# Second attention stage: a new table of steps for two heads on every engine, and a table of places for the neighbouring norms

## The chip, the cores and the metric

The kernel runs on one core of a Trainium2 chip. The metric is the device time of one execution in microseconds (us). A core has TensorE (PE, with its weight loads as PEld), VectorE (DVE), ScalarE (ACT), GpSimd (POOL) and SyncE (SP), each with an instruction stream of its own that it works off in order. A step that depends on another engine waits for a semaphore, and everything behind it in its stream waits with it.

## The reference

Six sublayers work on x of 2048 tokens by 256: a routed feed-forward, an attention, the same feed-forward again, a gated feed-forward, a second attention, the gated feed-forward again. Each reads a layer norm of x and adds its result to x. The change concerns the second attention:

```python
q = (x @ Wq.T).reshape(B, T, H, Dh)      # T 2048, H 16 heads, Dh 128
k = (x @ Wk.T).reshape(B, T, H, Dh)
v = (x @ Wv.T).reshape(B, T, H, Dh)
q = _apply_rope(q, cos, sin)
k = _apply_rope(k, cos, sin)
scores = jnp.einsum('bthd,bshd->bhts', q, k) * scale
scores = jnp.where(causal[None, None], scores, -jnp.inf)
attn = jax.nn.softmax(scores, axis=-1)
y = jnp.einsum('bhts,bshd->bthd', attn, v).reshape(B, T, H * Dh)
return y / 3.0 @ Wo.T
```

## The kernel before

The program runs six stages one behind the other; the fifth is `Attention1`, between two stages of the gated feed-forward. Every matrix product is made of three matmuls of two halves, a high one rounded and a low one that holds the rest (`products`, lines 166 to 168; the scores, line 1277).

The work of a head is cut into steps. The queries come in 16 tiles t of 128 rows, in 8 pairs g; the keys of tile t come in t // 4 + 1 chunks c of up to 512 columns. In the letters of the tables:

- p, `project`: q and k of a pair (12 matmuls of 256 columns into one of two ring banks), then four VectorE operations for the rotation (from line 2625);
- f, `finish`: ScalarE copies out the high halves (lines 2530, 2531), VectorE the low halves (2635, 2636);
- S, `score`: on TensorE three matmuls (1277) into one of four banks; on VectorE the chunk's peak (1290; 2323 for the last chunk of a tile, which is masked too), and then the tile's bias (2331);
- x, `exp`: ScalarE's exponential of a chunk (1311), which needs the bias of the whole tile and frees the bank. A chunk's scores wait for the exponential of four chunks earlier;
- T, `turn`: ScalarE rounds a chunk of probabilities (2305), GpSimd takes the rest (2336), SyncE transposes both by DMA (2346). There are eight rooms for this, and three rooms for the turned probabilities of a pair;
- s, `pv`: products (g, j) of a pair's probabilities with block j of the values, into one of two y banks;
- y, `round`: ScalarE's high half of y (2553) and VectorE's low half (2666);
- o, `out`: TensorE's product with Wo (6 matmuls), ScalarE's scaling by the softmax sums (2562), GpSimd's addition to x (2705);
- v, `values`, once for two heads (12 matmuls into the ring; 2538, 2655); i, `invert`, the reciprocals of the sums; b and u, `bound` and `share`, scales for values and Wo (2642; 2646, 2650), which pass through GpSimd (2682); q, w, l the splitting of weights, and Q, W, L on SyncE their loads.

A head has 40 score chunks, 25 of 512 columns, 7 of 384, 7 of 256 and one of 128, with three matmuls each, and 72 products of three matmuls, 64 over 256 columns and 8 over 128.

The order is written out by hand. `TABLE` (line 2079) holds for each engine a string of letters that stands for two heads; `plan_order` reads it ten times over, and each letter takes the next step of its kind. `LEAD` says with which step each letter begins in the first reading, so it shifts a kind of work against the others: `"s": -21` on `pe` lets the products trail the scores. The waits come from the data and the rooms and are placed with each step, whatever the order. `with_norms` then puts in the steps of two neighbouring norms: `stats`, `scale` and `flip` of the last chunk of this stage's own norm, which fall into head 0, `next_stats`, `next_scale` and `next_flip` of the first two chunks of the following stage's norm, and `ahead`, two pieces of its weights, which fall into head 15. It finds their places by rules. `pe_score` is called for each `score`:

```python
if old := self.old_chunk[key]:
    pe.wait_ge(*self.p_done[old])
```

## Time and profile before

| | us |
|---|---|
| median of three runs (1786.37 to 1788.04) | 1787.68 |
| the profiled execution | 1790.02 |
| its span, first to last instruction | 1788.2 |
| TensorE busy in the span | 1673.8 |
| VectorE busy | 1380.6 |
| ScalarE busy | 1246.9 |
| GpSimd busy | 1081.2 |
| mean granted TensorE clock | 0.989 |

The second attention takes two thirds of the span: its first matmul starts at 476.53 us, the next stage's first at 1687.63. Busy times of TensorE have modelled ends, and a matmul's window overlaps the next one's, so its starts say more than its durations.

### The profile page before, as it was taken

What the parts mean: (1) busy time and instruction counts of PE and PEld (TensorE: products, weight loads), DVE (VectorE), ACT (ScalarE), POOL (GpSimd) and SP (SyncE); (2) the same over time, 40 slices, a digit from 0 to 9 for tenths busy, and PEclk for the clock granted to TensorE, in tenths of its full rate; (3) what the DMA queues carried; (4) which work ended last, traced back from release to release, by engine and by line L of the source; (5) the groups of instructions that cost most, each with busy time, mean ns of one, the idle gap of its engine ahead of it and who ended that gap; (6) DMA issues with size and microseconds to landing.
All of it is one profiled execution on the core that took longest, in us unless ns stands there. A gap on an engine that the chain in (4) does not pass through costs nothing.

```text
span 1788.2 us, 37269 instructions
## 1 busy us (share of the span) xinstructions
PE 1673.8 (94%) x11566; PEld 1440.7 (81%) x11566; DVE 1380.6 (77%) x3611; ACT 1246.9 (70%) x3255; POOL 1081.2 (60%) x1098
## 2 busy tenths in 40 slices
PE   6998988999789999999999999999999999999899
PEld 4777876778778788888888878878888887887788
DVE  7358865475698898988989889898888988989453
ACT  4335642345378879779788897887978888788742
POOL 2633114553247767767685786776778678677732
PEclk9999999999999999999999999999999999999999
DMA  8843047640048867786696876868779587786700
GB/s 294 242 79 48 13 163 230 150 100 1 15 79 149 127 119 136 119 145 122 117 157 97 153 124 121 138 118 136 131 120 152 100 145 125 119 142 121 134 21 28
DMA packets 636133, 215.96 MB, mean 121 GB/s; under 512 B 587296, under 2 KB 622752, under 8 KB 635808
## 3 DMA queue, kind: packets, MB, share of 16 engines
q1 hardware_dynamic: 625568, 200.71, 58.3%
q0 software_dynamic: 10368, 12.85, 4.4%
q8 instruction: 95, 1.56, 0.4%
q14 instruction: 102, 0.84, 0.2%
HBM read 51.06 MB, written 19.80 MB: 40 GB/s over the span
## 4 chain that ended last, share of the span: by engine, by line
PE 60%; DVE 17%; ACT 8%; issue 7%; DMA 4%; POOL 3%; SPq 0%; ACTq 0%; POOLq 0%; DVEq 0%
PE phase_scores L1277 16%; PE phase_y L166 6%; PE phase_y L168 6%; PE phase_y L167 6%; ACT phase_p L1311 4%; PE phase_ring L166 4%; PE phase_ring L168 4%; PE phase_ring L167 4%; DVE phase_peaks L1290 2%; DVE phase_ring L2628 2%; PE phase_up_ps L166 2%; DMA y_rows<-phase_out,phase_rows 2%; DVE phase_crossed L2626 2%; DVE phase_crossed L2625 2%; PE phase_up_ps L168 2%
## 5 line engine op out<-in xcount | busy, mean ns | idle before, releaser
L2336 POOL TENSOR_TENSOR phase_split<-phase_p,phase_split 128x512 f16<-128x512 f32 (+3 forms) x640 | 650.4, 1016 | 183.1 <-ACT phase_split L2305 139.3
L1311 ACT ACTIVATE phase_p<-phase_scores,phase_bias 128x512 f32<-128x512 f32 (+3 forms) x680 | 417.7, 627 | 75.8 <-DVE phase_bias L2331 52.9
L2305 ACT ACTIVATE phase_split<-phase_p 128x512 f16<-128x512 f32 (+3 forms) x640 | 338.7, 578 | 4.8 <-DMA phase_pt<-phase_split 3.3
L1290 DVE TENSOR_REDUCE phase_peaks<-phase_scores 128x1 f32<-128x512 f32 (+1 forms) x408 | 267.1, 668 | 69.1 <-PE phase_scores L1277 66.3
L166 PE MATMUL phase_y<-phase_pt,phase_v_hi 128*128 128x256 f16 (+1 forms) x1152 | 308.0, 269 | 2.7 <-DMA phase_pt<-phase_split 2.0
L167 PE MATMUL phase_y<-phase_pt,phase_v_hi 128*128 128x256 f16 (+1 forms) x1152 | 307.6, 267 | 0.0
L168 PE MATMUL phase_y<-phase_pt,phase_v_lo 128*128 128x256 f16 (+1 forms) x1152 | 304.2, 267 | 0.0
L1277 PE MATMUL phase_scores<-phase_k_hi,phase_q_hi 128*128 128x512 f32 (+3 forms) x640 | 255.4, 399 | 38.4 <-ACT phase_p L1311 25.7
L2705 POOL TENSOR_TENSOR sb_x<-sb_x,phase_part 128x512 f32<-128x512 f32 x128 | 164.0, 1282 | 127.4 <-ACT phase_part L2562 121.7
L1277 PE MATMUL phase_scores<-phase_k_hi,phase_q_lo 128*128 128x512 f32 (+3 forms) x640 | 233.1, 364 | 0.0
L1277 PE MATMUL phase_scores<-phase_k_lo,phase_q_hi 128*128 128x512 f32 (+3 forms) x640 | 233.0, 364 | 0.0
L1277 PEld LDWEIGHTS phase_scores<-phase_k_hi,phase_q_hi 128*128 128x128 f32 x640 | 121.5, 190 | 75.5 <-ACT phase_p L1311 31.7
L166 PEld LDWEIGHTS phase_y<-phase_pt,phase_v_hi 128*128 128x128 f16 x1152 | 112.2, 97 | 53.0 <-issue 35.7
L166 PE MATMUL phase_ring<-sb_xt_hi,late_qk_hi 128*128 128x256 f32 x512 | 146.2, 286 | 0.0
L167 PE MATMUL phase_ring<-sb_xt_lo,late_qk_hi 128*128 128x256 f32 x512 | 142.8, 279 | 0.0
L168 PE MATMUL phase_ring<-sb_xt_hi,late_qk_lo 128*128 128x256 f32 x512 | 142.7, 279 | 0.0
L1311 ACT ACTIVATION_READ_ACCUMULATOR phase_p<-phase_scores,phase_bias 128x1 f32 x680 | 141.2, 208 | 0.0
L1277 PEld LDWEIGHTS phase_scores<-phase_k_hi,phase_q_lo 128*128 128x128 f32 x640 | 121.6, 190 | 17.4
L1277 PEld LDWEIGHTS phase_scores<-phase_k_lo,phase_q_hi 128*128 128x128 f32 x640 | 122.4, 191 | 7.9
L168 PEld LDWEIGHTS phase_y<-phase_pt,phase_v_lo 128*128 128x128 f16 x1152 | 112.8, 98 | 11.6
L167 PEld LDWEIGHTS phase_y<-phase_pt,phase_v_hi 128*128 128x128 f16 x1152 | 113.4, 98 | 9.3
L2323 DVE CUSTOM_DVE_ANT_0 phase_scores<-phase_scores,sb_hide,phase_peaks 128x256 f32<-128x256 f32 x192 | 113.4, 591 | 5.9 <-DVE phase_peaks L2320 0.3
(313 smaller groups left out, 4485.8 us busy)
## 6 DMA issues: line engine op xcount, KB each, us to landing
phase_pt<-phase_split SPq DMA_TRANSPOSE x640, 3.3
y_rows<-phase_zero SPq DMA_DIRECT2D x16, 512.0 KB, 7.6
phase_e_up<-expert_up SPq DMA_DIRECT2D x16, 352.0 KB, 4.2
phase_e_dn<-expert_down SPq DMA_DIRECT2D x16, 256.0 KB, 5.4
xn_rows<-phase_ln_xn SPq DMA_DIRECT2D x8, 512.0 KB, 2.9
sb_x<-y_rows POOLq DMA_DIRECT2D x8, 512.0 KB, 6.2
late_raw_qk<-qk SPq DMA_DIRECT2D x16, 256.0 KB, 3.2
phase_logits_t<-expert_up SPq DMA_DIRECT2D x8, 352.0 KB, 4.2
```

Source lines behind the costliest of these rows:

```text
L166: pe.matmul(out, left_hi[c], r_hi, start=first and c == 0, stop=False)
L167: pe.matmul(out, left_hi[c], r_lo, start=False, stop=False)
L168: done = pe.matmul(out, left_lo[c], r_hi, start=False, stop=last and c == n - 1)
L1277: done = pe.matmul(self.scores[:, at:at + n], a, b, start=k == 0, stop=k == len(pairs(n)) - 1)
L1290: dve.tensor_reduce(peak, scores, AX.X, ALU.max).then_inc(*self.peaked.one)
L1311: act.activation(self.p_room(act, key)[:, 0:width], self.scores[:, at:at + width], ACT.Exp, bias=self.bias[:, t % 2:t % 2 + 1], accum_out= ...
L2305: act.activation(hi, value, ACT.Copy).then_inc(*self.t_hi.one)
L2323: dve.tensor_tensor_reduce(scores, scores, self.core.hide[:, CH - w:], 1.0, before, ALU.add, ALU.max, top).then_inc(*self.peaked.one)
L2336: pool.tensor_tensor(lo, value, hi, ALU.subtract).then_inc(*self.t_lo.one)
L2625: dve.tensor_tensor(self.crossed[0:32], both[32:64], self.wide(slice(96, 128), g), ALU.mult)
L2626: dve.tensor_tensor(self.crossed[32:64], both[0:32], self.wide(slice(64, 96), g), ALU.mult).then_inc(*self.crossing.one)
L2705: pool.tensor_tensor(rows, rows, self.part[:, g % 2], ALU.add).then_inc(*self.added.one)
```

## The change

It replaces the five strings of `TABLE` and the numbers of `LEAD`, and puts a table `PLACES` in place of the rules of `with_norms`. Each string holds the same letters, as often as before, in another order; what each engine executes stays the same. A row of `PLACES` names a step and the norm steps that follow it directly (-1 is the last head). The strings are cut here to the first row of `pe`:

```diff
 TABLE = {
-    "pe": ("SSpSsssSpssssssssssssSSSSpsssssSSSsvSooSpSSsSsvssoSSSpssssSsSSsvvoSsSSpssSSsssSssssvvoSSSSsssssssssSSSSsvvoSSSSp"
...
+    "pe": ("sSpssSSsssSssoSspsssSSsssSvosSsSsSsssSsssssspSosSsvSSSssvSSposSSvsSSsssssoSSvsSpSsvSssssSovsSSSssSsspSSSSosvsSsSS"
...
 LEAD = {
-    "pe": {"S": 0, "s": -21, "p": 2, "v": 0, "o": -2, "b": 1},
-    "act": {"x": 0, "T": -1, "f": 1, "y": -2, "v": 0, "o": -2, "l": 0, "q": 1, "w": 1},
-    "dve": {"f": 1, "S": 0, "i": 0, "p": 2, "y": -2, "v": 0, "b": 1, "u": 1},
-    "pool": {"T": -2, "o": -2, "l": 0, "q": 1, "w": 1, "b": 1},
-    "sp": {"T": -5, "L": 1, "Q": 2, "W": 2},
+    "pe": {"S": 0, "s": -27, "p": 3, "v": 0, "o": -3, "b": 1},
+    "act": {"x": -10, "T": -12, "f": 0, "v": 0, "y": -4, "o": -5, "q": 1, "w": 1, "l": 0},
+    "dve": {"S": -2, "p": 2, "f": 0, "v": 0, "y": -3, "i": -2, "b": 1, "u": 0},
+    "pool": {"T": 4, "o": -1, "q": 1, "w": 1, "l": 0, "b": 1},
+    "sp": {"T": 26, "Q": 2, "W": 2, "L": 2},
+}
+PLACES = {
+    "pe": ((("project", 0, 1), ("flip", 3, 0), ("flip", 3, 1)),
+           (("pv", -1, 6, 1), ("next_flip", 0, 0)),
+           (("pv", -1, 7, 7), ("next_flip", 0, 1)),
+           (("out", -1, 7), ("next_flip", 1, 0), ("next_flip", 1, 1)),),
...
+    "dve": (((), ("stats", 3)),
+           (("project", 0, 0), ("scale", 3)),
+           (("finish", 0, 0), ("flip", 3, 0), ("flip", 3, 1)),
...
+    "sp": (),
 }
@@ with_norms @@
+        for after, *steps in PLACES[engine]:
+            at = order.index((after[0], after[1] % NH, *after[2:])) + 1 if after else 0
+            order[at:at] = steps
         return order
```

VectorE in the middle of the stage, head 7 (odd), from the first peak of tile 8 on. L2625 to L2630 are the rotation of a projection, L2666 is the low half of y, L2323 and L2331 end the tile. Before:

```order
L1290 TENSOR_REDUCE phase_peaks<-phase_scores 128x1
L2642 TENSOR_SCALAR phase_bound<-phase_ring 128x1
L2625 TENSOR_TENSOR phase_crossed<-phase_ring,late_rope 32x512
L2626 TENSOR_TENSOR phase_crossed<-phase_ring,late_rope 32x512
L2628 TENSOR_TENSOR phase_ring<-phase_ring,late_rope 64x512
L2630 TENSOR_TENSOR phase_ring<-phase_ring,phase_crossed 64x512
L1290 TENSOR_REDUCE phase_peaks<-phase_scores 128x1
L2666 TENSOR_TENSOR phase_y_lo<-phase_y,phase_y_hi 128x256
L2320 TENSOR_REDUCE phase_peaks<-phase_peaks 128x1
L2323 ISA phase_scores,phase_top<-phase_scores,sb_hide,phase_peaks 128x256
L2323 ISA phase_top 128x1
L2331 TENSOR_SCALAR phase_bias<-phase_top 128x1
```

With the change (lines behind `with_norms` lie six lower, so L2619 is L2625):

```order
L1290 TENSOR_REDUCE phase_peaks<-phase_scores 128x1 x2
L2660 TENSOR_TENSOR phase_y_lo<-phase_y,phase_y_hi 128x256
L2314 TENSOR_REDUCE phase_peaks<-phase_peaks 128x1
L2317 ISA phase_scores,phase_top<-phase_scores,sb_hide,phase_peaks 128x256
L2317 ISA phase_top 128x1
L2325 TENSOR_SCALAR phase_bias<-phase_top 128x1
L1327 TENSOR_REDUCE phase_inv<-phase_sums 128x1
L1329 RECIPROCAL phase_inv<-phase_inv 128x1
L2660 TENSOR_TENSOR phase_y_lo<-phase_y,phase_y_hi 128x256
L2619 TENSOR_TENSOR phase_crossed<-phase_ring,late_rope 32x512
L2620 TENSOR_TENSOR phase_crossed<-phase_ring,late_rope 32x512
```

The projection, which stood between the first and the second chunk of tile 8, follows the tile and two low halves of y.

TensorE in head 7, from product (3, 7), the last of pair 3, on: `phase_pt` with `phase_v` are products, `phase_wo` with `phase_y` an output, `phase_ring` a projection. Before:

```order
L166 MATMUL phase_y<-phase_pt,phase_v_hi 128x128
L167 MATMUL phase_y<-phase_pt,phase_v_hi 128x128
L168 MATMUL phase_y<-phase_pt,phase_v_lo 128x128
L166 MATMUL phase_y<-phase_wo_hi,phase_y_hi 128x256
L167 MATMUL phase_y<-phase_wo_lo,phase_y_hi 128x256
L168 MATMUL phase_y<-phase_wo_hi,phase_y_lo 128x256
L166 MATMUL phase_y<-phase_wo_hi,phase_y_hi 128x256
L167 MATMUL phase_y<-phase_wo_lo,phase_y_hi 128x256
L168 MATMUL phase_y<-phase_wo_hi,phase_y_lo 128x256
L166 MATMUL phase_y<-phase_wo_hi,phase_y_hi 128x256
L167 MATMUL phase_y<-phase_wo_lo,phase_y_hi 128x256
L168 MATMUL phase_y<-phase_wo_hi,phase_y_lo 128x256
```

With the change:

```order
L166 MATMUL phase_y<-phase_pt,phase_v_hi 128x128
L167 MATMUL phase_y<-phase_pt,phase_v_hi 128x128
L168 MATMUL phase_y<-phase_pt,phase_v_lo 128x128
L166 MATMUL phase_ring<-sb_xt_hi,late_qk_hi 128x256
L167 MATMUL phase_ring<-sb_xt_lo,late_qk_hi 128x256
L168 MATMUL phase_ring<-sb_xt_hi,late_qk_lo 128x256
L166 MATMUL phase_ring<-sb_xt_hi,late_qk_hi 128x256
L167 MATMUL phase_ring<-sb_xt_lo,late_qk_hi 128x256
L168 MATMUL phase_ring<-sb_xt_hi,late_qk_lo 128x256
```

Before, the output of pair 2 and then that of pair 3 follow the last product of pair 3, and tile 13's scores come behind them. Now a projection of head 8 follows, three products of pair 4 come behind it, then tile 13; pair 3's output stands behind product (4, 9).

VectorE at the start of the stage: L241 and L245 are the statistics of the last norm chunk, L2642 the bound, L2646 and L2650 the share, L2625 the first projection. Before:

```order
L241 BN_STATS phase_ln_stats<-sb_x 128x6 x4
L245 BN_AGGR phase_ln_mv<-phase_ln_stats 128x2 x4
L2642 TENSOR_SCALAR phase_bound<-phase_ring 128x1
L2646 TENSOR_SCALAR phase_spread<-phase_v_scale 128x1
L2650 RECIPROCAL phase_wo_scale<-phase_spread 128x1
L2625 TENSOR_TENSOR phase_crossed<-phase_ring,late_rope 32x512
L2626 TENSOR_TENSOR phase_crossed<-phase_ring,late_rope 32x512
```

With the change:

```order
L241 BN_STATS phase_ln_stats<-sb_x 128x6 x4
L245 BN_AGGR phase_ln_mv<-phase_ln_stats 128x2 x4
L2636 TENSOR_SCALAR phase_bound<-phase_ring 128x1
L2619 TENSOR_TENSOR phase_crossed<-phase_ring,late_rope 32x512
L2620 TENSOR_TENSOR phase_crossed<-phase_ring,late_rope 32x512
L2622 TENSOR_TENSOR phase_ring<-phase_ring,late_rope 64x512
L2624 TENSOR_TENSOR phase_ring<-phase_ring,phase_crossed 64x512
L281 TENSOR_TENSOR phase_ln_tmp<-phase_ln_rstd 128x4
```

The share step has gone behind later work, and the norm's scale follows the first projection.

## Rows read from the trace of the kernel before

**Rows 1.** The page, busy us, share of the span and instructions of each engine.
```profile
PE 1673.8 (94%) x11566; PEld 1440.7 (81%) x11566; DVE 1380.6 (77%) x3611; ACT 1246.9 (70%) x3255; POOL 1081.2 (60%) x1098
```

**Rows 2.** Windows: busy us (instructions) by engine, granted clock, DMA share, GB/s.
```profile
524.00:1664.00 1140.00, 1096.85 (x8128) 956.56 (x8127) 986.49 (x2610) 953.12 (x2611) 831.22 (x793) 1.00 0.76 129
```

**Rows 3.** The chain that ended last: start us, us, what.
```profile
652.08 1.92 PE phase_scores L1277 x9
...
1540.97 1.92 PE phase_scores L1277 x9
```

**Rows 4.** Timeline of TensorE: start us, us, engine, line, operation, count [idle before].
```profile
1089.74 0.27 PE L166 MATMUL phase_y<-phase_pt,phase_v_hi 128*128 128x256 f16 x1
...
1090.61 0.27 PE L168 MATMUL phase_y<-phase_pt,phase_v_lo 128*128 128x256 f16 x1
...
1091.25 0.28 PE L1277 MATMUL phase_scores<-phase_k_hi,phase_q_hi 128*128 128x256 f32 x1
...
1091.60 0.40 PE L1277 MATMUL phase_scores<-phase_k_hi,phase_q_hi 128*128 128x512 f32 x1
...
1092.29 0.28 PE L1277 MATMUL phase_scores<-phase_k_hi,phase_q_hi 128*128 128x256 f32 x1
```

**Rows 5.** Waits of TensorE, 524 to 1664: us in total, times, longest.
```profile
PE phase_scores L1277 <- ACT phase_p L1311: 25.1, 54, 1.0
...
PE phase_y L166 <- DVE phase_y_lo L2666: 17.3, 25, 1.0
```

**Rows 6.** Timeline of TensorE, waits in one pair of heads.
```profile
1035.88 0.38 PE L166 MATMUL phase_y<-phase_wo_hi,phase_y_hi 128*128 128x256 f32 x1 [1.03 <-DVE phase_y_lo L2666]
...
1037.53 0.50 PE L1277 MATMUL phase_scores<-phase_k_hi,phase_q_hi 128*128 128x512 f32 x1 [0.70 <-ACT phase_p L1311]
...
1057.59 0.38 PE L166 MATMUL phase_y<-phase_wo_hi,phase_y_hi 128*128 128x256 f32 x1 [0.58 <-DVE phase_y_lo L2666]
...
1102.48 0.47 PE L1277 MATMUL phase_scores<-phase_k_hi,phase_q_hi 128*128 128x512 f32 x1 [0.98 <-ACT phase_p L1311]
```

**Rows 7.** Timeline of VectorE and ScalarE around those waits.
```profile
1032.08 0.68 DVE L2625 TENSOR_TENSOR phase_crossed<-phase_ring,late_rope 32x512 f32<-32x512 f32 x1
...
1034.94 0.56 DVE L1290 TENSOR_REDUCE phase_peaks<-phase_scores 128x1 f32<-128x384 f32 x1
...
1036.51 0.15 DVE L2331 TENSOR_SCALAR phase_bias<-phase_top 128x1 f32<-128x1 f32 x1
...
1056.30 0.38 ACT L2553 ACTIVATE phase_y_hi<-phase_y 128x256 fp32r<-128x256 f32 x1
...
1057.12 0.41 DVE L2666 TENSOR_TENSOR phase_y_lo<-phase_y,phase_y_hi 128x256 fp32r<-128x256 f32 x1
```

**Rows 8.** Timeline: tile 13 of head 7, last score, reduction, first exponential.
```profile
1061.13 0.28 PE L1277 MATMUL phase_scores<-phase_k_hi,phase_q_lo 128*128 128x256 f32 x1
...
1062.18 0.49 DVE L2323 CUSTOM_DVE_ANT_0 phase_scores<-phase_scores,sb_hide,phase_peaks 128x256 f32<-128x256 f32 x1
...
1062.95 0.69 ACT L1311 ACTIVATE phase_p<-phase_scores,phase_bias 128x512 f32<-128x512 f32 x1 [0.18 <-DVE phase_bias L2331]
```

**Rows 9.** Timeline of TensorE and VectorE, start of the stage.
```profile
487.19 0.47 PE L1277 MATMUL phase_scores<-phase_k_hi,phase_q_hi 128*128 128x128 f32 x1 [7.31 <-DVE phase_k_lo L2636]
...
480.21 0.15 DVE L2646 TENSOR_SCALAR phase_spread<-phase_v_scale 128x1 f32<-128x1 f32 x1 [2.12 <-POOL phase_v_scale L2682]
...
480.59 0.68 DVE L2625 TENSOR_TENSOR phase_crossed<-phase_ring,late_rope 32x512 f32<-32x512 f32 x1
```

**Rows 10.** Timeline and waits of TensorE, end of the stage.
```profile
1670.86 0.56 PE L166 MATMUL phase_y<-phase_wo_hi,phase_y_hi 128*128 128x256 f32 x1 [1.96 <-DVE phase_y_lo L2666]
...
PE phase_y L166 <- DMA phase_pt<-phase_split: 2.0, 1, 2.0
```

**Rows 11.** Line 2346, the transposes: ns min/median/max, and who waited for them.
```profile
L2346 SPq DMA_TRANSPOSE phase_pt<-phase_split x640: 1171/1259/2544, 492.1 to 1680.5; - x160
...
  ACT phase_split L2305: 3.3, 7
```

More of the change, by code:

```diff
@@ new lines @@
+    "act": ("xTxoyTTTxxTxxTfToTfxxTyTxxxfxToTTTxfxyTxxxxTfvTTxxTToyxxTlyfovTxxvTTxTxTxxoyfvxxTTxTovTyxTxqTxfTTTvxxxxToyvTxxxT"
+           "xTTTTTxxxTTxvfToyTxxxxTfTxToyfTTwxxTfTTxoTxxTfxxTTxxTTTxyTxyTxoTxlfoyxTxxTTxoqyfTxxyTTTxoxTxTxTofTyxxxTxTTTxx"),
+    "dve": ("SfSifpSyiSSiifpSSifSSiuySpSiSifSviSypSSfSSivySvSpSiSySfSvSiSiSyvpSSfSviSSSSivySSSiSpSSiSfvSypiSfpSySfipSiSfiSiSp"
+           "SSiSbfSiSiSSySiypSSfSypSSiSfySiSySpSSSiSfiySSSiSpSSiSySpSS"),
+    "pool": "TTTloTTTTToTTTTTTTqTTTTToToTTTTTTTTToTTTTwTTToTTToTTTTTTTTToloTTTqToTTTTTooTTTTTTTTTTTTTTTTboTTTToToTo",
@@ L2089 @@
+    "sp": "TTTTTTTTTTTTTTTTTQTTTTTTTTTTTTTTTTTTTTTTTTTTLTTTTTQTTTTWTTTTTTTTTTTTTTTTTTTTTTTTTTTLT",
 }
 LEAD = {
[5 rows of a table removed]
[5 rows of a table added]
+}
[4 more added lines that the diff above has]
+           (("out", -1, 7), ("next_flip", 1, 0), ("next_flip", 1, 1)),),
+    "act": ((("finish", 0, 0), ("scale", 3), ("flip", 3, 0), ("flip", 3, 1)),
+           (("exp", -1, 13, 0), ("next_scale", 0)),
+           (("round", -1, 6), ("next_flip", 0, 0), ("ahead", 0), ("ahead", 1)),
+           (("out", -1, 6), ("next_flip", 0, 1)),
+           (("round", -1, 7), ("next_scale", 1), ("next_flip", 1, 0)),
+           (("out", -1, 7), ("next_flip", 1, 1)),),
+    "dve": (((), ("stats", 3)),
+           (("project", 0, 0), ("scale", 3)),
+           (("finish", 0, 0), ("flip", 3, 0), ("flip", 3, 1)),
+           (("score", -1, 12, 1), ("next_stats", 0)),
+           (("round", -1, 4), ("next_scale", 0)),
+           (("invert", -1, 15), ("next_stats", 1), ("next_flip", 0, 0)),
+           (("round", -1, 6), ("next_flip", 0, 1), ("next_scale", 1)),
+           (("round", -1, 7), ("ahead", 0), ("ahead", 1), ("next_flip", 1, 0), ("next_flip", 1, 1)),),
+    "pool": ((("bound", 0), ("stats", 3)),
+           (("turn", -1, 11, 2), ("next_stats", 0)),
+           (("out", -1, 4), ("next_stats", 1)),),
+    "sp": (),
@@ L2238, in with_norms @@
     def with_norms(self, engine, order):
-        def after(anchor, *steps):
-            if anchor in order:
-                order[order.index(anchor) + 1:order.index(anchor) + 1] = steps
-        late, h = NCH - 1, NH - 1
-        score = {"pe": "score", "act": "exp", "dve": "score"}.get(engine)
-        if engine in ("dve", "pool"):
-            order.insert(0, ("stats", late))
-        if engine in ("act", "dve"):
-            after((score, 0, 1, 0), ("scale", late))
-            at = order.index(("round", h, G - 1))
-            order[at:at] = [("ahead", m) for m in range(2)]
-        if engine in ("pe", "act", "dve"):
-            flips = [("flip", late, 0), ("flip", late, 1)]
-            if engine == "act" and order.index(("finish", 0, 2)) < order.index(("exp", 0, 2, 0)):
-                at = order.index(("finish", 0, 2))
-                order[at:at] = flips
-            else:
-                after((score, 0, 2, 0), *flips)
-        for c in AHEAD:
-            flips = [("next_flip", c, k) for k in range(HK)]
-            if engine == "dve":
-                later = [(score, h, NT - 1, NCH - 1)] * c
-                after(max([("round", h, 2 * c + 5), *later], key=order.index), *flips)
-                after(max([("round", h, 2 * c + 4), *later], key=order.index), ("next_scale", c))
-                after(("round", h, 2 * c + 3), ("next_stats", c))
-            elif engine == "act":
-                later = [(score, h, NT - 1, NCH - 1)] * c
-                after(max([("round", h, 2 * c + 5), *later], key=order.index), *flips)
-                after(max([("round", h, 2 * c + 4), *later], key=order.index), ("next_scale", c))
-            elif engine == "pool":
-                after(max([("out", h, 2 * c + 2)] + [("turn", h, NT - 1, NCH - 1)] * c, key=order.index), ("next_stats", c))
-            elif engine == "pe":
-                after(("out", h, 2 * c + 4), *flips)
+        for after, *steps in PLACES[engine]:
+            at = order.index((after[0], after[1] % NH, *after[2:])) + 1 if after else 0
+            order[at:at] = steps
         return order
```

11 lines of the change are left out of this document (3 added, 8 removed).

## The prediction

> **What bounds the kernel now.** I began with the busy shares: TensorE is busy 94% of the span, VectorE 77%, ScalarE 70% [rows 1]. They are averages over six stages, so I cut the span: in the second attention stage, from 524 to 1664 us, TensorE is busy 1096.85 of 1140 us, VectorE 986, ScalarE 953, GpSimd 831, at a granted clock of 1.00 [rows 2]. The stage repeats itself every two heads. In the chain of waits the same piece of scores comes at 652.08 and, six pairs of heads later, at 1540.97 [rows 3]: 148.15 us a pair.
>
> Is that TensorE's limit? By busy time almost. But the ends of matmuls are modelled and overlap their successors, so I counted from start to start in a stretch without waits. A product of probabilities and values takes 0.109 us (eight of them between 1089.74 and 1090.61); a score matmul of 256 columns takes 0.117 (three from 1091.25), one of 512 columns 0.23 (three from 1091.60) [rows 4]. I give 0.175 to 384 columns, 0.055 to half a product, and 0.117 to the projections, values and outputs, which have 256 columns of the same type too. A pair of heads has 384 whole and 48 half products, 150, 42, 42 and 6 scores of 512, 384, 256 and 128 columns, 288 matmuls of projections and values and 96 of outputs, all counted in the code. That is 41.9 + 2.6 + 34.5 + 7.4 + 4.9 + 0.6 + 33.7 + 11.2, about **137 us of streaming**. So TensorE loses about **11 us in each pair of heads**, 85 us over the 7.7 pairs from 524 to 1664.
>
> Where? The waits view of that stretch charges TensorE's idle time to ScalarE's exponentials (25.1 us, 54 times) and to VectorE's low half of y (17.3 us, 25 times) [rows 5]; idle time between modelled ends is less than what the starts lose. One pair shows the pattern [rows 6]: at 1035.88 an output step waits 1.03 us for the low half of y, at 1037.53 a score 0.70 for the bank that an exponential must free, at 1057.59 an output again, at 1102.48 a score.
>
> A rule of the Trainium skill bears on this. First the rows: TensorE's idle time by its busy row is 43 us in the stretch [rows 2], by starts it is 85. The Trainium skill, Perfetto Trace Analysis, section Identifying the Most-Contended Engine, says that matmul busy time is no good measure of how near the limit TensorE is, because pipelined matmuls look smaller in the trace. By the busy row the steady part could give back at most 43 us, half of what I look for below. The count of starts sides with the page.
>
> **The change, part by part.** Every engine executes the same instructions; only their order moves. So each term is a wait.
>
> *Steady part.* (a) VectorE had head 7's sixth projection inside tile 8, before its second chunk: four operations from 1032.08 on, so that chunk's peak starts at 1034.94 and the tile's bias at 1036.51 [rows 7]. The waits at 1035.88 and 1037.53 hang on it. In the new order the projection stands behind the tile and behind pair 7's low half. (b) Pair 3's output stood right behind pair 2's, 0.7 us of TensorE work behind its own pair's last product, while the round trip over ScalarE's copy (0.38 us) and VectorE's subtraction (0.41) [rows 7] costs about 1.2 us even with both free (my estimate: the two, and three crossings between engines like the 0.18 ahead of the exponential [rows 8], partly overlapped). Over the 16 outputs of a pair of heads, the work between last product and output is 0.7, 0.7, 1.4, 1.6, 1.8, 1.8 and 2.1 us for the seven shortest in the old order; in the new one 2.1, 2.1, 2.5, 2.9, then 4 and more. (c) The work between a tile's last score and the score that needs its first exponential was 1.9 us at its shortest (tile 8 to 9 of odd heads, the place of (a)); that place has 4.0 now. Tile 13 to 14 goes the other way, from 2.9 to 2.0 (even heads) and 2.2 (odd). That chain costs 2.4: the last score starts at 1061.13 and lasts 0.12, the exponential ends at 1063.64 [rows 8]. This leaves 0.4 and 0.2 us to wait.
>
> I also laid ScalarE's and VectorE's own work, in order, against TensorE's work between each event and the step that needs its outcome. The old order overruns by up to 1.6 us on ScalarE and 2.1 on VectorE, at the places of the waits; in the new one I find none above 0.1 beside tile 13's. Fetches of weights are moved past transposes in SyncE's queue, but each is still issued several tiles before its use; I cost them at nothing, and without that cover each would cost its landing once a head.
>
> What is left: 0.6 us for tile 13 and about 2 us a pair of slips that no distance explains, 2.7 in all. The bounds are 0.5 (no slips) and half of today's 11. Gain 8.4 x 7.7 = **64.7 us**.
>
> *Start.* TensorE waits 7.31 us before the first score at 487.19; VectorE stood 2.12 us of that at the share step, for GpSimd, and began the first projection at 480.59 [rows 9]. Now only the bound step stands before it, so it can begin at about 478.1. In return the last norm chunk's scale and flips come before the second projection's low halves, on ScalarE and VectorE too, and the scores behind them. I take **2.4** gained, nearly the whole of those 2.5 us, since the flips are only moved; bounds -4 and +6.
>
> *End.* Output 5 of the last head stood directly behind its last product and waited 1.96 us [rows 10]; it has 4.0 us of work ahead of it now. The last output, which had output 6 and two flips ahead of it, now stands directly behind the last product and pays the round trip of 1.2. The wait of 2.0 us for the last transposes [rows 10] stays, since the same 12.1 us of TensorE work lie between the last score and the product that needs them. **0.8** gained; bounds -3 and +4.
>
> Sum: 64.7 + 2.4 + 0.8 = 67.9. The profiled execution took 1790.0 us, so 1722.1; the median of the runs is 2.3 lower, so **1720 us**.
>
> On the floor of 137 us the rows say 0.23 us for 512 columns. The Trainium skill, TensorE: Matmul & The Clock Gate, section Back-to-back issue gap, gives 131 ns sustained. By it the 150 wide scores of a pair would cost 15 us less, so TensorE would not be at its limit even after the change. The rows decide; nothing of the sum rests on this.
>
> **The rivals.** *Half comes back (0.19).* The distances use durations of undisturbed rows, and a wait that goes makes the next engine late: VectorE would be busy 92% of a 140 us period. If half of the loss stays, the gain is 5.5 x 7.7 = 42, so 1746. For it: several places of the new order have under 0.4 us to spare. Against: all of today's large waits sit at places that are covered now.
>
> *Nothing comes back (0.04).* The 11 us could be TensorE's own, from switching between kinds of work; the new order switches 150 times a pair, the old 111. Then 1788. Against: the score of 256 columns behind another kind at 1091.25 pays nothing [rows 4].
>
> *Slower (0.05).* The products trail the scores by six steps more. There are three rooms for turned probabilities, so SyncE's transpose of tile 8 waits for product (1, 3) of the same head, with all later transposes behind it. TensorE's work from tile 8's last score to that product grows from 8.8 to 10.4 us in odd heads and from 7.6 to 9.2 in even ones. The way to the transpose is about 4.5: 2.4 to the exponential's end, then ScalarE's split and GpSimd's. SyncE's wait so grows to 5.9 and 4.7 us. ScalarE may be eight splits ahead, at 1.26 us a transpose [rows 11] a cover of 10 us; but it has already been caught seven times, for 3.3 us in all [rows 11]. If the waits reached TensorE in full, 10.6 + 2.7 would replace 11: 2.3 x 7.7 = 18 us slower, 1806. It decides once such a wait and the backlog behind it pass those 10 us.
>
> **How the numbers follow.** The forecast's case gets 0.72 and reaches from 1703 (0.5 left a pair) to 1740 (5 left). With most of the half case the range is 1703 to 1752; outside lie the cases nothing and slower, 0.09, a third of the half case and a little below, under 0.2 together. Faster by over 0.2% (about what a measurement of this kernel can tell from no change) 0.91; within it 0.04; slower 0.05.
>
> **What would show it.** Right: the scores' piece returns every 140 us instead of 148; TensorE's waits for exponentials and y are under 12 us in the steady part instead of 42; its DMA share goes from 0.76 to about 0.80, VectorE to 92%; at the start VectorE's first projection begins near 478. Wrong: a period above 144, ScalarE's splits waiting for transposes by tens of us, or TensorE waiting for transposes in every head.

## The result: 1722.0 us, and the profile after

The changed kernel takes 1721.99 us (median of 4 runs, 1718.1 to 1724.86), the kernel before 1787.12 (4 runs, 1786.37 to 1788.04). The ratio is 0.9635, with a 95% interval of 0.9617 to 0.9652. The forecast was 1720.0 in a range of 1703 to 1752. The profiled execution took 1724.86 us, and its rows are these.

The page of the changed kernel: busy us, share of the span and instructions of each engine; the chain that ended last, by engine.

```profile
PE 1648.0 (96%) x11566; PEld 1418.2 (82%) x11566; DVE 1373.5 (80%) x3611; ACT 1238.2 (72%) x3255; POOL 1081.6 (63%) x1098
...
PE 83%; DVE 8%; ACT 3%; issue 3%; DMA 2%; POOL 1%; SPq 0%; ACTq 0%; POOLq 0%; DVEq 0%
```

The busy times of VectorE, ScalarE and GpSimd are those of before within 1% [rows 1], as only the order moves. The steady part of the second attention, as windows and as TensorE's and SyncE's waits:

```profile
524.00:1600.00 1076.00, 1070.96 (x8128) 934.54 (x8127) 978.59 (x2611) 945.46 (x2613) 834.60 (x795) 1.00 0.79 137
```

```profile
PE phase_scores L1277 <- ACT phase_p L1311: 5.0, 3, 3.8
```

```profile
SPq L2340 <- POOL phase_split L2330: 501.4, 451, 6.7
SPq L2338 <- PE phase_y L168: 43.8, 22, 4.8
```

The waits for the low half of y are gone from this stretch, and of those for exponentials 5.0 us are left where 25.1 were [rows 5]. All three of these stand at 1584.53 or behind it, at the end of the stage, and 3.8 of the 5.0 is the first of them: from 524 to 1584 the view lists no wait of TensorE. VectorE is busy 91% of the stretch, DMA 0.79. In the chain of waits the same piece of scores (of another cut than in [rows 3], since the order is another) returns so:

```profile
661.49 1.40 PE phase_scores L1277 x6
...
800.36 1.40 PE phase_scores L1277 x6
...
939.41 1.40 PE phase_scores L1277 x6
```

That is 138.9 us for a pair of heads where it was 148.15 [rows 3]. To split the gain into places I used the same three steps in both traces: the stage's first matmul, the first score of tile 8 in head 1 and in head 15, and the first matmul of the next stage. Timeline of TensorE, first the kernel before:

```profile
476.53 0.35 PE L2460 MATMUL phase_ring<-late_power,phase_ones 128*128 128x1 f32 x2 [1.33 <-POOL phase_ones L2671]
...
585.93 0.47 PE L1277 MATMUL phase_scores<-phase_k_hi,phase_q_hi 128*128 128x512 f32 x1
...
1622.96 0.47 PE L1277 MATMUL phase_scores<-phase_k_hi,phase_q_hi 128*128 128x512 f32 x1
...
1687.63 0.40 PE L166 MATMUL phase_up_ps<-sb_xt_hi,phase_up_hi 128*128 128x512 f32 x1
```

and the changed one:

```profile
476.77 0.35 PE L2454 MATMUL phase_ring<-late_power,phase_ones 128*128 128x1 f32 x2 [1.34 <-POOL phase_ones L2665]
...
582.63 0.47 PE L1277 MATMUL phase_scores<-phase_k_hi,phase_q_hi 128*128 128x512 f32 x1
...
1555.03 0.47 PE L1277 MATMUL phase_scores<-phase_k_hi,phase_q_hi 128*128 128x512 f32 x1
...
1622.21 0.48 PE L166 MATMUL phase_up_ps<-sb_xt_hi,phase_up_hi 128*128 128x512 f32 x1
```

| piece | before | after | gained | by the forecast's terms |
|---|---|---|---|---|
| first matmul to tile 8 of head 1 | 109.4 | 105.9 | 3.5 | 0.4 pairs x 8.4 + 2.4 = 5.8 |
| seven pairs of heads | 1037.0 | 972.4 | 64.6 | 7 x 8.4 = 58.8 |
| tile 8 of head 15 to the next stage | 64.7 | 67.2 | -2.5 | 0.3 x 8.4 + 0.8 = 3.3 |
| sum | 1211.1 | 1145.4 | 65.7 | 67.9 |

So the sum is nearly that of the forecast, but the steady part gave 6 us more and the end 6 us less. In a second execution of the changed kernel the pieces are 104.5, 972.3 and 68.3 us: the first and the last move by over 1 us between executions, the middle one doesn't. What went wrong at the end stands in two places of the changed kernel's timeline. The first, around the first score of tile 13 of the last head:

```profile
1580.22 1.41 DVE L241 BATCH_NORM_STATS2 phase_ln_stats<-sb_x 128x6 f32<-128x256 f32 x4 [1.13 <-POOL sb_x L2699]
...
1583.42 0.15 DVE L2325 TENSOR_SCALAR phase_bias<-phase_top 128x1 f32<-128x1 f32 x1
1583.61 0.69 ACT L1311 ACTIVATE phase_p<-phase_scores,phase_bias 128x512 f32<-128x512 f32 x1 [2.81 <-DVE phase_bias L2325]
...
1584.53 0.47 PE L1277 MATMUL phase_scores<-phase_k_hi,phase_q_hi 128*128 128x512 f32 x1 [3.79 <-ACT phase_p L1311]
```

VectorE stands 1.13 us for GpSimd in the next stage's statistics, and works 1.8 on them (1.41 and the 0.38 of L245 behind it), before it may finish tile 12. ScalarE so stands 2.81 us and TensorE 3.79. The window from 1.5 us behind it:

```profile
1586.00:1589.40 3.40, 3.40 (x14) 2.32 (x13) 1.85 (x6) 1.82 (x6) 2.91 (x6) 0.51 0.87 59
```

The granted clock, the third column from the right, is 0.51 for these 3.4 us: about 1.7 us more are lost. The kernel before had a wait of 1.96 us in this piece [rows 10], with 3.4 us at 0.50 behind it as well. The second place is the last output, right behind its product as foreseen, which waits 2.29 us for the low half of y in this execution (0.93 in the second one of the same kernel).

### The profile page after: what moved, and what is told of

Its sections match the earlier page's. It is cut to its first block, busy times and chain, and to the rows that moved or that the text cites. A ratio compares the mean times of both kernels' runs of the same rounds, so it can differ in the third digit from the quotient of the medians.

```text
span 1723.1 us, 37269 instructions
## 1 busy us (share of the span) xinstructions
PE 1648.0 (96%) x11566; PEld 1418.2 (82%) x11566; DVE 1373.5 (80%) x3611; ACT 1238.2 (72%) x3255; POOL 1081.6 (63%) x1098
## 4 chain that ended last, share of the span: by engine, by line
PE 83%; DVE 8%; ACT 3%; issue 3%; DMA 2%; POOL 1%; SPq 0%; ACTq 0%; POOLq 0%; DVEq 0%
PE phase_scores L1277 22%; PE phase_y L166 9%; PE phase_y L167 9%; PE phase_y L168 9%; PE phase_ring L166 5%; PE phase_ring L168 5%; PE phase_ring L167 5%; PE phase_banks L777 2%; PE phase_up_ps L166 2%; PE phase_up_ps L168 2%; PE phase_up_ps L167 2%; PE phase_banks L796 2%; PE phase_banks L166 1%; PE phase_banks L168 1%; PE phase_banks L167 1%
## 5 line engine op out<-in xcount | busy, mean ns | idle before, releaser
L2299 ACT ACTIVATE phase_split<-phase_p 128x512 f16<-128x512 f32 (+3 forms) x640 | 345.5, 577 | 0.0
L166 PEld LDWEIGHTS phase_y<-phase_pt,phase_v_hi 128*128 128x128 f16 x1152 | 112.6, 98 | 79.2 <-issue 63.8
L166 PE MATMUL phase_ring<-sb_xt_hi,late_qk_hi 128*128 128x256 f32 x512 | 150.8, 295 | 4.4 <-DVE phase_k_lo L2630 4.4
L1277 PEld LDWEIGHTS phase_scores<-phase_k_hi,phase_q_lo 128*128 128x128 f32 x640 | 120.9, 189 | 17.3
L2556 ACT ACTIVATE phase_part<-phase_y,phase_inv 128x256 f32<-128x256 f32 x256 | 108.9, 489 | 15.9 <-PE phase_y L168 15.8
```

Of the source, the lines that this page charges most:

```text
L166: pe.matmul(out, left_hi[c], r_hi, start=first and c == 0, stop=False)
L1277: done = pe.matmul(self.scores[:, at:at + n], a, b, start=k == 0, stop=k == len(pairs(n)) - 1)
L2299: act.activation(hi, value, ACT.Copy).then_inc(*self.t_hi.one)
L2556: done = act.activation(self.part[:, g % 2, n, :], self.y_bank(key)[:, n * H:(n + 1) * H], ACT.Copy, scale=self.inv[:, h % 2, t:t + 1])
```

## The experiments

Twelve runs in three sets, each on one chip with the kernel before. The sets differ by up to 0.6% (medians of before 1785.2, 1788.3 and 1796.3 us), so I compare ratios to before; 0.001 is 1.8 us. The changed kernel ran again in the first set only, and its ratio there stands for it in the other two.

### The changed kernel again, and the end of the stage

No edit in the first. 

> The changed kernel once more, as the measure beside which the others of this set are read. Its four times so far lie between 1718.1 and 1724.9 us. I expect 1719 to 1724, a ratio of 0.962 to 0.965.

Measured: 1721.5 us (1717.4 to 1723.85), ratio 0.9637 (0.9612 to 0.9663). It is the measure below.

In the second, three places of the table of norms:

```
-           (("exp", -1, 13, 0), ("next_scale", 0)),
+           (("turn", -1, 13, 3), ("next_scale", 0)),
-           (("score", -1, 12, 1), ("next_stats", 0)),
+           (("round", -1, 3), ("next_stats", 0)),
-           (("turn", -1, 11, 2), ("next_stats", 0)),
+           (("turn", -1, 12, 3), ("next_stats", 0)),
```

> The first step of the next stage's statistics goes from inside tile 12 of the last head to behind pair 3's low half on VectorE, with GpSimd's and ScalarE's steps after it. Theory A (TensorE's 3.95 us before score 13 of the last head, and the half clock that follows it at 1586, come from VectorE standing in that step for GpSimd): the stall goes below 0.5 us and the half clock with it, the time falls by 4 to 7 us against the changed kernel. Theory B (tile 12's chain is late anyway, by ScalarE's queue): the stall stays at 2 us or more and the time within 2 us of the changed kernel's. Theory C: the step is late at its new place, and its chain shows up in front of the last products or the next stage: the time rises.

Measured: 1717.5 us (1715.95 to 1718.8), ratio 0.9611 (0.9585 to 0.9636), 4.6 us below the changed kernel by the ratios and 4.0 by the medians; the two intervals overlap by 0.0024. Its timeline at tile 13 and at the last pair's first product and last output:

```profile
1578.07 0.47 PE L1277 MATMUL phase_scores<-phase_k_hi,phase_q_hi 128*128 128x512 f32 x1 [0.86 <-ACT phase_p L1311]
...
1604.85 0.37 PE L166 MATMUL phase_y<-phase_pt,phase_v_hi 128*128 128x256 f16 x1 [4.16 <-DMA phase_pt<-phase_split]
...
1613.69 0.39 PE L166 MATMUL phase_y<-phase_wo_hi,phase_y_hi 128*128 128x256 f32 x1 [0.93 <-DVE phase_y_lo L2660]
```

The wait of 3.79 is 0.86, so theory A names the right cause, though it gave less than 0.5. But the wait for transposes grew from 2.1 to 4.16: TensorE comes to the last transposes sooner, and they are no sooner there. Part of what the first place gave went there, with the half clock, which this execution has at that wait. Theory C does not show, since the time fell.

The third run adds this, on VectorE:

```
-           (("round", -1, 6), ("next_flip", 0, 1), ("next_scale", 1)),
-           (("round", -1, 7), ("ahead", 0), ...
+           (("round", -1, 6), ("next_flip", 0, 1)),
+           (("round", -1, 7), ("next_scale", 1), ("ahead", 0), ...
```

> As before it, and the step of the next norm's scale goes on VectorE from before to behind the low half of the last pair. Theory A (the 2.45 us before the last output come from VectorE standing in that step): a further 1 to 1.5 us, 1713 to 1718 us in all, the best of these kernels. Theory B (the next stage needs that scale at once, so what the output gains the first matmul of the next stage loses): no difference from the kernel with the first move alone.

Measured: 1715.2 us (1713.26 to 1718.11), ratio 0.9595 (0.957 to 0.962). It is the fastest here of the kernels that leave no work out, 7.5 us below the changed one by the ratios (6.3 by the medians). What the second move adds to the first is 2.9 us by the ratios (2.3 by the medians), less than the intervals can tell, and its last output waited the same 0.93 us as without it: the wait of 2.3 at that output, seen in one execution of the changed kernel, is 0.9 in both. So theory A is not shown for this move, and B not refuted.

### Places of the new order undone one by one

On TensorE only, output 3 of odd heads goes back:

```
+        if engine == "pe":
+            for n in range(1, NH, 2):
+                order.remove(("out", n, 3))
+                order.insert(order.index(("pv", n, 3, 7)) + 1, ("out", n, 3))
```

> In the new order output 3 of odd heads goes back on TensorE to directly behind its own pair's last product; the other engines keep their order. Theory A (distances): the round trip over ScalarE's copy and VectorE's subtraction has no work beside it now and costs its whole 1.2 us, or up to 2 if ScalarE or VectorE come to it late, in each of 8 odd heads: 8 to 16 us slower than the changed kernel. Theory B (TensorE's loss is its own, from switching kinds of work): a switch less per pair of heads, so no change or a little faster.

Measured: 1753.9 us (1752.76 to 1756.65), ratio 0.9818 (0.9792 to 0.9844): 32 us slower than the changed kernel, twice the top of what theory A gave. Timeline of TensorE, and windows from its wait on:

```profile
1034.21 0.58 PE L166 MATMUL phase_y<-phase_wo_hi,phase_y_hi 128*128 128x256 f32 x1 [2.22 <-DVE phase_y_lo L2664]
...
1177.56 0.58 PE L166 MATMUL phase_y<-phase_wo_hi,phase_y_hi 128*128 128x256 f32 x1 [2.23 <-DVE phase_y_lo L2664]
```

```profile
1034.20:1035.20 1.00, 0.99 (x4) 0.99 (x5) 0.00 (x0) 1.00 (x5) 0.93 (x1) 0.50 1.04 193
...
1037.20:1038.20 1.00, 1.00 (x9) 0.94 (x9) 0.00 (x0) 0.00 (x0) 0.92 (x2) 0.87 1.07 200
```

Two sizes were off. The round trip is 2.2 us here and not 1.2, because ScalarE and VectorE come to it behind other work of their own (ScalarE's copy starts at 1032.62, VectorE's subtraction, behind the low halves of q and k and an inversion, at 1033.75). And the granted clock is 0.50 for about 3.4 us behind the wait. The period, 1034.21 to 1177.56, is 143.35 instead of 138.9, that is 4.4 us for one wait of 2.2: 2.2 idle, 1.7 of half clock, and 0.35 in a later score. By the steps of the table the seven pairs of heads take 29.4 us more than in the changed kernel. In the eighth odd head the wait is 5.15 us, but there the changed kernel waited too, and the end of the stage takes about 3 us more. Theory B would have had it a little faster, and falls: the loss is a wait, not the changing of kinds of work.

Next, the sixth projection of odd heads:

```
+        if engine in ("pe", "dve"):
+            for n in range(1, NH, 2):
+                order.remove(("project", n, 5))
+                place = order.index(("score", n, 8, 0)) + (engine == "dve")
+                order.insert(place, ("project", n, 5))
```

> In the new order the sixth projection of odd heads goes back into tile 8 (on TensorE before the tile's first score, on VectorE behind it); this is place (a) of the prediction, undone. Theory A (distances): TensorE's work between tile 8's last score and the score behind it that needs its exponential is 2.6 us instead of 4.0, against a chain of 1.9 with the projection's four operations (2.9 us) ahead of it: 1 to 2 us lost in each of 8 odd heads, 8 to 16 us slower than the changed kernel. Where such a wait passes 2 us in one piece the clock falls for 3.4 us behind it, as in the run with output 3 put back, which adds 1.7 each: up to 30 us. Theory B (the other places of the new order do the work, this one had cover): within 4 us of the changed kernel.

Measured: 1762.2 us (1756.35 to 1763.56), ratio 0.9841 (0.9817 to 0.9864): 36 us slower than the changed kernel, above theory A's top of 30. Timeline of VectorE and TensorE, tile 8 of head 7:

```profile
1014.30 0.69 DVE L1290 TENSOR_REDUCE phase_peaks<-phase_scores 128x1 f32<-128x512 f32 x1 [1.29 <-PE phase_scores L1277]
1015.02 0.68 DVE L2624 TENSOR_TENSOR phase_crossed<-phase_ring,late_rope 32x512 f32<-32x512 f32 x1
...
1018.36 0.41 DVE L2665 TENSOR_TENSOR phase_y_lo<-phase_y,phase_y_hi 128x256 fp32r<-128x256 f32 x1
...
1018.83 0.39 PE L166 MATMUL phase_y<-phase_wo_hi,phase_y_hi 128*128 128x256 f32 x1 [2.77 <-DVE phase_y_lo L2665]
```

The place decides, as theory A has it, but by another road: it isn't the exponential that is late first but the low half of y, queued behind the projection's four operations (1015.02 to 1017.85) on VectorE. TensorE waits 2.77 us at once and again gets the half clock: its windows from 1018.8 and from 1022.2 on show 0.69 and 0.64. The expectation puts a line for that at waits of 2 us, which no run shows (last section). Seven periods of this run are 143.5 to 145.0 us. So each of the two places alone, undone in the new order, takes back about half of the change's gain of 65 us. What such a place costs belongs to the order around it: in the kernel before the same projection in the same tile cost TensorE waits of 1.03 and 0.70 us [rows 6].

### The same places mended in the kernel before

```
+        if engine == "dve":
+            for n in range(1, NH, 2):
+                order.remove(("project", n, 5))
+                order.insert(order.index(("finish", n, 5)), ("project", n, 5))
+        if engine == "act":
+            for n in range(1, NH, 2):
+                order.remove(("finish", n, 5))
+                order.insert(order.index(("exp", n, 8, 2)) + 1, ("finish", n, 5))
```

> The kernel before, with one thing moved: the sixth projection of odd heads goes behind tile 8 on VectorE, and ScalarE's copies that wait for it (finish) behind tile 8's exponentials. Theory A: the stalls of 1.19, 0.94 and 0.71 us between 1034 and 1039 us in the trace of the kernel before are this one place, so 2 to 3 us a pair of heads come back: 16 to 24 us faster than before, 1763 to 1771 us. Theory B (the loss is handed on to the next tight place, the output behind it): under 8 us faster.

Measured: 1794.9 us (1793.07 to 1799.56, 9 runs), ratio 1.0041 (1.0029 to 1.0054): 7 us slower than before, against both theories, though B comes nearer. In the profiled execution 1.7 us of the 7 are clock: its steady part has three stretches of 3.4 us at half clock, that of the kernel before two. Timeline of TensorE in head 7, the stretch of [rows 6]:

```profile
1034.24 0.50 PE L1277 MATMUL phase_scores<-phase_k_hi,phase_q_hi 128*128 128x512 f32 x1 [0.38 <-ACT phase_p L1311]
...
1037.15 0.36 PE L166 MATMUL phase_y<-phase_wo_hi,phase_y_hi 128*128 128x256 f32 x1 [0.88 <-POOL phase_wo_lo L2605]
1038.38 0.50 PE L1277 MATMUL phase_scores<-phase_k_hi,phase_q_hi 128*128 128x512 f32 x1 [0.28 <-DVE phase_k_lo L2644]
1041.72 0.50 PE L1277 MATMUL phase_scores<-phase_k_hi,phase_q_hi 128*128 128x512 f32 x1 [0.95 <-ACT phase_p L1311]
```

The wait of 1.03 at the output is gone and the 0.70 is 0.38. In their place TensorE waits for the weights of the next output, which GpSimd hands over no sooner, for the low half of k, and 0.95 for tile 9's exponential. In ScalarE's and VectorE's timelines one sees why: the projection and the copies that belong to it now follow one another without anything between, so each of the two engines waits for the other. (Columns as in the rows above.)

```profile
1036.87 0.38 ACT L2538 ACTIVATE phase_q_hi<-phase_ring 128x256 fp32r<-128x256 f32 x1 [0.82 <-DVE phase_ring L2638]
...
1037.57 0.42 DVE L2643 TENSOR_TENSOR phase_q_lo<-phase_ring,phase_q_hi 128x256 fp32r<-128x256 f32 x1 [0.72 <-ACT phase_k_hi L2539]
```

The next run adds two outputs to it (places for TensorE and ScalarE):

```
+        places = {"pe": (("score", 13, 2), ("score", 2, 0)),
+                  "act": (("exp", 13, 1), ("exp", 2, 0))}
+        ...   ("out", n, 3) behind the first, ("out", n - 1, 5) behind the second, n odd
```

> As before it, and output 3 of odd heads and output 5 of even heads, both 0.7 us behind their pair's last product in the old order, go three or two tiles' steps later on TensorE, with ScalarE's copies of them. Theory A (each place is worth what its stalls in the trace of before add up to, 1.2 and 0.8 us a pair of heads): a further 12 to 16 us, about 1750 us; so two places make half of the change's gain. Theory B (TensorE only meets the next wait sooner): no more than with the projection alone. Half of the change comes from places that no single wait marks in either case.

Measured: 1806.0 us (1804.4 to 1809.17), ratio 1.0094 (1.0076 to 1.0112), 17 us slower than before, so theory A has the wrong sign. TensorE's waits, 524 to 1664 us:

```profile
PE phase_scores L1277 <- ACT phase_p L1311: 34.7, 57, 1.7
PE phase_scores L1277 <- DVE phase_k_lo L2653: 13.0, 15, 1.7
PE phase_y L166 <- POOL phase_wo_lo L2614: 7.0, 8, 0.9
```

No output waits for a low half of y any more (17.3 us in [rows 5]), and the sum of the waits is 55 instead of 42, as in theory B's "meets the next wait sooner". Later outputs took their place in front of scores and made ScalarE and VectorE late for those. I gave these steps one new place each and looked for no better one, so this shows that these mends don't pay, not that none would.

```
+        if engine == "dve":
+            for n in range(1, NH, 2):
+                order.remove(("project", n, 5))
+                order.insert(order.index(("score", n, 8, 2)) + 1, ("project", n, 5))
```

> The kernel before, with the same projection moved on VectorE alone; ScalarE's copies of it stay ahead of tile 8's exponentials in its queue. Theory A (in-order queues: a step moved on one engine holds the next engine at its old place): ScalarE stands until VectorE is through with tile 8 and the projection, so no exponential of tile 8 frees a bank before that, and TensorE loses 3 us or more in each odd head, with a fall of the clock behind it: 25 to 60 us slower than before. Theory B (VectorE's place is what counts): faster, as with both moved.

Measured: 1805.5 us (1804.31 to 1811.85), ratio 1.0091 (1.0075 to 1.0108): 16 us slower, by theory A's road, with one wait of 3.5 to 3.8 us for an exponential in each odd head and the half clock around each, but under its 25, since the waits that it replaces (1.03, 0.70 and a further 0.44 in head 7) are to be taken off, as I had not done. Timeline of TensorE in head 7:

```profile
1047.06 0.50 PE L1277 MATMUL phase_scores<-phase_k_hi,phase_q_hi 128*128 128x512 f32 x1 [3.56 <-ACT phase_p L1311]
```

### SyncE, rooms, and work taken from TensorE

The kernel before, with SyncE's row of the table replaced by the new one (`TABLE["sp"]`, `LEAD["sp"]`). 

> The kernel before with SyncE's order alone taken from the new table. Before, SyncE stood behind fetches of weights for GpSimd and ScalarE, up to 8.8 us at once and 102 us in all, with the transposes behind it. Theory A (my forecast costed the moved fetches at nothing: TensorE never waited for a transpose in the steady part): within 3 us of before. Theory B (transposes behind those fetches filled the split rooms and so held ScalarE): 5 to 15 us faster. Theory C: the new order of transposes doesn't fit the old order of splits, and it is slower by 5 us or more.

Measured: 1792.6 us (1789.75 to 1801.59, 10 runs), ratio 0.9993 (0.9977 to 1.001). Theory A holds. In the kernel before SyncE stood 58 us in front of one kind of fetch, with the transposes behind it, and taking that away gained nothing that can be measured (in its place SyncE waits longer for products):

```profile
SPq L2403 <- POOL phase_wo_lo L2597: 58.1, 7, 8.8
```

Then the changed kernel with `SPLIT_ROOMS` 6 instead of 8. 

> The changed kernel with six rooms for splits instead of eight, so that ScalarE can be six transposes ahead of SyncE and not eight (a cover of 7.6 us instead of 10). In the changed kernel SyncE waits 22 times for products of pairs before, 43.8 us in all and up to 4.8 at once. Theory A (those waits, which the slower rival named, stay inside the cover, and TensorE is far enough behind the scores): under 4 us slower than the changed kernel, ScalarE's splits waiting a few us in all. Theory B (the cover is nearly used up): ScalarE waits for rooms in most heads, its exponentials behind it are late, and the time rises by 10 to 40 us.

Measured: 1740.0 us (1738.02 to 1741.9), ratio 0.9694 (0.9673 to 0.9715), 10 us slower than the changed kernel, at B's lower end. In its waits SyncE stands for products as before (44.4 us), but ScalarE, which in the changed kernel never waited for a room, does now (the first row), and TensorE has a wait at a projection that it didn't have (the second):

```profile
ACT phase_split L2299 <- DMA phase_pt<-phase_split: 13.7, 23, 2.2
```

```profile
PE phase_ring L166 <- DVE phase_k_lo L2630: 5.4, 8, 1.0
```

So the slower rival's mechanism is real: with eight rooms it costs nothing that shows, with six 10 us.

Last, 128 matmuls of 0.23 us left out, in the changed kernel and in the one before:

```
+                    few = c == 0 and t >= 8
-                    return [(q_hi, k_hi), (q_hi, k_lo), (q_lo, k_hi)]
+                    return [(q_hi, k_hi), (q_hi, k_lo), (q_lo, k_hi)][:2 if few else 3]
```

> The changed kernel without the third matmul (low half of q by high half of k) of the first 512-key piece of scores of tiles 8 to 15 in every head: 128 matmuls of 0.23 us, 29.4 us of TensorE's work; that part of the scores is left out. Theory A (TensorE is the bound in nearly every place): 24 to 30 us faster than the changed kernel. Theory B (VectorE and ScalarE, at 91% and 88%, are all but the bound, and the distances that cover the round trips shrink with the work): under 15 us faster, with waits for exponentials or y back on TensorE.

> The kernel before with the same 128 matmuls left out (29.4 us of TensorE's work; that part of the scores is left out). Theory A (its 11 us a pair of heads are waits whose cover is TensorE's own work, and which grow when that work shrinks): 10 to 22 us faster than before, less than the changed kernel gains by the same. Theory B (the 11 us are TensorE's own, from switching between kinds of work): the whole 29 us.

Measured: 1710.9 us (1709.5 to 1712.92), ratio 0.9534 (0.9514 to 0.9554), for the changed kernel, 18 us of the 29.4, between both theories. For the kernel before 1781.2 us (1777.97 to 1781.97), ratio 0.9926 (0.9907 to 0.9946), 13 us, inside A. The changed kernel's period is then 1158.01 - 1020.99 = 137.0 us (chain of waits, in two heads apart), where 3.7 us of work were taken out and 1.9 came off:

```profile
1020.99 1.85 PE phase_scores L1277 x8
...
1158.01 1.85 PE phase_scores L1277 x8
```

Its waits view for 524 to 1540 us has one row for TensorE, 0.5 us in all: the rest sits in slips of 0.1 to 0.2 us between starts, which that view does not show. So TensorE bounds the changed kernel, but something else is only about 2 us a pair behind it. That it is VectorE or ScalarE, busy 93% and 89% of this stretch, is likely and not shown.

## Why the prediction was right, step by step

*What bounds the kernel.* Right. TensorE's 11 us a pair were waits in an in-order queue: when the order covers them the period falls from 148.15 to 138.9, when one cover is taken away it goes back to 143 and more. The floor of 137 held too: 138.9 leaves 1.9. That the busy row underrates the loss was also right: 9.2 us a pair came back, where that row has 43 in the whole stretch, 5.6 a pair. But the reason that the prediction takes from the Trainium skill (Perfetto Trace Analysis, Identifying the Most-Contended Engine), that pipelined matmuls look smaller in the trace, would do the opposite. Here they look larger: the row has TensorE busy for 1097 us, and the starts give 137 x 7.7, about 1055.

*Steady part, 64.7 us for 7.7 pairs.* The mechanism was right, the size too small. Measured is 9.2 a pair, about 71 us. The term that was mis-sized is "0.6 us for tile 13 and about 2 us a pair of slips that no distance explains, 2.7 in all": 1.9 was left in all. And not all that came back was waits: 3.4 us of the 71 are clock (last section), for which the forecast had no term, since its 11 us a pair were put down to waits alone. Tile 13's 0.6 does not exist. The timeline of the changed kernel, tile 13's last score to the score that needs its exponential, in head 8:

```profile
1099.78 0.29 PE L1277 MATMUL phase_scores<-phase_k_hi,phase_q_lo 128*128 128x256 f32 x1
...
1100.22 0.49 DVE L2317 CUSTOM_DVE_ANT_0 phase_scores<-phase_scores,sb_hide,phase_peaks 128x256 f32<-128x256 f32 x1 [0.15 <-PE phase_scores L1277]
...
1101.06 0.69 ACT L1311 ACTIVATE phase_p<-phase_scores,phase_bias 128x512 f32<-128x512 f32 x1
...
1101.99 0.47 PE L1277 MATMUL phase_scores<-phase_k_hi,phase_q_hi 128*128 128x512 f32 x1
```

From the last matmul's 0.12 us, 1099.90, to the exponential's end at 1101.75 are 1.85 us, not 2.4, and the distance is 2.1. In [rows 8] VectorE began its reduction 1.05 us behind the start of that matmul, here 0.44: there it was still busy with an earlier peak. I had taken a row with a queue in it for the bare chain. Score 14 follows without a wait.

*Fetches at nothing.* Right: TensorE waits for no transpose in the steady part, and SyncE's order alone changed nothing in the kernel before.

*Start, 2.4 us (-4 to +6).* The size is inside its bounds, the mechanism was wrong. VectorE's first projection begins at 478.7 instead of 480.59 [rows 9], as foreseen, but the first score doesn't gain by it. It starts 12.65 us behind the stage's first matmul, where it was 10.66 before, because TensorE now has the norm's flips and a projection in front of it and stands at the flips for ScalarE's part of the norm. Timeline of TensorE:

```profile
483.56 1.94 PE L322 MATMUL phase_y<-sb_ident,phase_xn 128*128 128x128 f32 x8 [3.48 <-ACT phase_xn L315]
...
489.42 0.31 PE L1277 MATMUL phase_scores<-phase_k_hi,phase_q_hi 128*128 128x128 f32 x1
```

That is made up for soon, since work was only moved forward: the first score of tile 8 of head 0 starts 34.2 us behind the stage's first matmul, where it was 34.0 before (33.0 in the second execution of the changed kernel). So the start itself gave 0 to 1 us, and most of the 3.5 gained up to tile 8 of head 1 (4.9 in the second execution) is steady part. The terms gave 5.8. In the start TensorE also waits for projections, 2.05 us at 495.38 and 3.14 at 508.25. Which of the moved steps makes them late wasn't tried.

*End, +0.8 us (-3 to +4).* Wrong in sign: with 0.3 of the steady gain taken off, the last piece lost about 5 us, in the second execution about 6. The step that failed is one that I left out: of the end I costed the outputs and the last transposes, and not the places of the next stage's norm, one of which stands inside tile 12 on VectorE and waits for GpSimd. The run with those three places moved showed it, 4.6 us. Its wait of 3.79 us with the half clock behind it was in no term. That the forecast came within 2 us of the measured time is luck in part: the 6 us too few in the steady part and the 6 too many at the end cancel.

*Rivals.* "Half comes back" and "nothing comes back" did not occur (138.9 against 142.6 and 148). Yet the first one's reason, that a wait that goes makes the next engine late, is what the runs on the kernel before showed, at full size: two places mended there gave a loss of 17 us. The new table covers all of them at once. How the gain divides among its five strings was tried for SyncE's only, which gains nothing without the others. "Slower" did not occur, but its wait did: SyncE stood 43.8 us for products, 4.8 at most, where the rival gave 5.9 and 4.7; in the same stretch of the kernel before it stood 12.6, and 5.1 at most. The eight rooms covered all of it, and six do not. The rival's price, with 10 us of cover, was right about which side of the line the kernel is on.

## What to carry to other kernels

In an order of in-order queues, add up for each wait the work that lies between cause and use on every engine involved, and look at all places together. A step or two moved can hand the wait to the next place: the three such moves tried on the kernel before made it slower. It need not be so: three places of the norm, moved at the end of the changed kernel, took 4.6 us off by the ratios. Look hardest at the seams of stages, where a step of the next stage that waits for a third engine sits in front of this stage's critical work. And before counting a chain's length from a row, see that no engine in it was still busy with something else.

## What the runs showed of the hardware

Waits of TensorE can cost more than their length. At the waits of 2.22 us in the run with output 3 back (six of seven), of 2.77 + 0.46 with the projection back, of 3.5 to 3.8 with it moved on VectorE alone and of 3.79 at the end, the granted clock was about 0.5, that is 1.2 instead of 2.4 GHz, for about 3.4 us and in a few places twice that. The stretch begins at times behind the wait and at times within it. With that in view I went back to the kernel before. Its steady part has two such stretches that I had not seen in the mean of 1.00 [rows 2], both at the place of [rows 6] in other heads, where TensorE waits 1.03 and about 0.7 us one shortly after the other. Windows of one of them:

```profile
1332.00:1333.00 1.00, 0.33 (x3) 0.13 (x2) 0.99 (x4) 0.80 (x3) 0.92 (x2) 0.99 0.00 0
1333.00:1334.00 1.00, 0.97 (x2) 0.84 (x3) 0.76 (x2) 0.97 (x3) 0.47 (x2) 0.50 0.00 0
```

The changed kernel has none between 524 and 1584 us, so some 3.4 us of its gain are clock. But the same waits in the other heads of the kernel before had no such stretch behind them, nor had the first of the seven waits of 2.22 us:

```profile
605.71 0.39 PE L166 MATMUL phase_y<-phase_wo_hi,phase_y_hi 128*128 128x256 f32 x1 [2.22 <-DVE phase_y_lo L2664]
```

```profile
606.00:607.00 1.00, 1.00 (x11) 1.00 (x11) 0.00 (x0) 1.00 (x4) 0.92 (x2) 1.00 0.82 152
```

So the length of a wait alone doesn't decide it, and what else does stays open here. I counted the waits from 524 us on in all 14 traces. A stretch at half clock begins within the wait or up to 2 us behind it at all 24 waits of 2.77 us or more, at 8 of the 12 of 2.2 to 2.3 (the last output's 2.29 in the changed kernel has none), at 4 of the 12 of 1.9 to 2.1, and at none of the 15 of 1.3 to 1.75. Single waits shorter than that have none; where short ones have it, two or three stand within 4 us, as the two above do. As an estimate from these counts, a wait of 2.77 us or more costs its length and 1.7 us on top, and one near 2 us perhaps.
